# The down product of the first half of the tokens, turned round and in three float32r products

## The chip, the core and the metric

The kernel runs on one core of one Trainium2 chip. The metric is the device time of one execution in microseconds; three runs of the kernel before gave a median of 156.71 us (156.7 to 156.9). PE is TensorE, DVE is VectorE, ACT is ScalarE, POOL is GpSimd, SP is the queue engine that issues the DMAs.

## The reference

1024 tokens (4 batches of 256, 128 features) go through a cross attention over 1601 keys and then through a routed feed-forward part with 8 experts, 2 of them per token:

```
x = x + xattn(layernorm(x), ctx_1024, Wq, bq, Wk, bk, Wv, bv)
x = x + ffn(layernorm(x))

flat = hidden.reshape(B * S, H)
scores = softmax(flat @ router_weight.T + router_bias)
topk_w, topk_idx = top_k(scores, 2)
gu = einsum('th,ehn->ten', flat, gate_up_proj) + gate_up_bias
gate = minimum(gu[..., :I], 7.0);  up = clip(gu[..., I:], -7.0, 7.0)
act = (up + 1.0) * gate * sigmoid(gate * 1.702)
down = einsum('tei,eih->teh', act, down_proj) + down_bias
out = (take(down, topk_idx) * topk_w).sum(axis=1)
```

H is 128 and I is 256. All is float32.

## The kernel before

The tokens are eight tiles of 128, in two halves of four tiles (512 tokens). The attention goes tile by tile; its last tile overlaps the start of the feed-forward part. That part computes every expert for every token, and gives the experts that a token did not choose the weight 0. It is cut into 16 steps: four pairs of experts, and in each pair four steps (`PAIR_STEPS`), both experts for the first half of the tokens (k = 0, 1) and then both for the second (k = 2, 3). The first pair and the last are written out, the two in the middle are a hardware loop on every engine (`Fori`).

One step is:
- `gate_up` on PE: four groups (gate and up, each for two halves `ih` of the hidden features) of three float32r matmuls with 512 tokens streaming (`three`: high by high, high by low, low by high), into four PSUM banks S. The weights' high and low parts (`w_hi`, `w_lo`) are made by DVE one pair ahead, in the steps k = 2, 3.
- `silus` and `ups` on ACT: S with its bias into `gate` (it lies in `keysT_sb`) and `up` in SBUF, per `ih`.
- `clip_ups` and `product` on DVE: the clip of up, and gate by up into `act_t` (it lies in `xT` for even steps and in `act_odd` for odd ones).
- `down` on PE: for each token tile two float32 matmuls with the tile of `act_t` as the loaded weights and 128 columns of the down weights streaming; the tokens come out on the partitions. A float32 matmul is two passes in the trace. The result lies in the PSUM bank T0 or T1.
- `scale_y` on ACT: T by the routing weight of each token (per partition, `w_scaled`) into `y_sb` (it lies in `xn2`); `add_expert` on POOL: into `x1`.

The order on each engine is written out by hand. PE does the down product of step s, then gate_up of step s + 2. ACT and DVE go in step order. The routing of the second half (softmax, comparison of experts, weights) is on DVE between the products of steps 2 and 3, with a power operation on POOL for the exponentials. The biases of the down product are added as one product of the routing weights (turned by `transpose_weights`, copied by `copy_wT`) with `db_sb`, in `routed_bias`, into the banks O and M.

## Time and profile before

| | |
|---|---|
| runs, median | 156.71 us |
| profiled execution | 156.96 us |
| its span, first to last instruction | 155.2 us |
| PE busy | 149.2 us (96%) |
| PEld (weight loads) | 136.0 us |
| DVE busy | 103.2 us |
| ACT busy | 100.8 us |
| POOL busy | 49.8 us |
| granted TensorE clock | 1.000 |

The span is shorter than the profiled execution's time, since the time also holds what lies before the first and behind the last instruction. Busy times are of one engine each and overlap. An operation's recorded duration is a little longer than the distance at which the next one of its engine can follow.

### The profile page before, as it was taken

To read this page: it belongs to the slowest core of one execution; us is meant where nothing else is said; L and a number is where in the kernel's file an instruction comes from. 1 tells how busy PE (TensorE), PEld (TensorE's weight loads), DVE (VectorE), ACT (ScalarE), POOL (GpSimd) and SP (SyncE) were. 2 spreads that over 40 slices of the span, in tenths; PEclk is the share of its full clock that TensorE was granted. 3 is DMA by queue.
4 is the path that set the end of the run, shared out by engine and by line. 5 is a ranking of instruction groups with operands and counts; after the bars stand their busy time and mean duration, and the time that the engine had idled before them with its cause. 6 is when DMAs were issued, how large, how long until landed. Compare 5 with 4: busy or idle time off the path is not lost.

```text
span 155.2 us, 3023 instructions
## 1 busy us (share of the span) xinstructions
PE 149.2 (96%) x1004; PEld 136.0 (88%) x1004; DVE 103.2 (66%) x288; ACT 100.8 (65%) x205; POOL 49.8 (32%) x49
## 2 busy tenths in 40 slices
PE   7998799999999999999999999999999999999993
PEld 7988699999999999989988888788888888887892
DVE  0668958386859595963683899957654377552773
ACT  3183878657484736468866656957788677779450
POOL 1356529243505300210067643312333321233020
PEclk9999999999999999999999999999999999999999
DMA  4979999700000000000000000000000000000022
GB/s 116 371 292 404 388 401 384 225 1 4 0 2 0 4 0 0 4 0 2 0 0 4 0 0 0 0 4 0 2 0 0 0 0 0 0 4 0 4 68 68
DMA packets 5909, 10.69 MB, mean 69 GB/s; under 512 B 380, under 2 KB 3080, under 8 KB 5896
## 3 DMA queue, kind: packets, MB, share of 16 engines
q1 hardware_dynamic: 4968, 10.00, 17.9%
q10 hardware_dynamic: 928, 0.53, 1.2%
q8 instruction: 7, 0.11, 0.3%
q14 instruction: 6, 0.05, 0.1%
HBM read 10.00 MB, written 0.52 MB: 68 GB/s over the span
## 4 chain that ended last, share of the span: by engine, by line
PE 78%; DVE 10%; POOL 4%; ACT 3%; issue 3%; DVEq 0%
PE T L1147 14%; PE O L1041 13%; PE S L944 11%; PE S L946 10%; PE S L945 10%; PE T L1025 6%; PE S L951 3%; POOL ex L309 2%; DVE xT L847 2%; DVE up L838 1%; PE S L1147 1%; DVE w_lo L779 1%; DVE sc L631 1%; ACT pr L419 1%; POOL rstd L287 1%
## 5 line engine op out<-in xcount | busy, mean ns | idle before, releaser
L838 DVE TENSOR_SCALAR up<-up 128x512 f32<-128x512 f32 x32 | 13.9, 434 | 24.7 <-ACT up L504 24.7
L350 POOL TENSOR_TENSOR x<-x,xn 128x512 f32<-128x512 f32 x13 | 17.3, 1331 | 38.6 <-ACT xn L524 38.6
L427 ACT ACTIVATE pT<-T 128x512 f32<-128x512 f32 (+1 forms) x32 | 15.4, 513 | 18.4 <-PE T L1025 18.4
L524 ACT ACTIVATE xn<-T,w_scaled 128x128 f32<-128x128 f32 x56 | 16.1, 374 | 17.2 <-PE T L1147 14.1
L944 PE MATMUL S<-x_hi,w_hi 128*128 128x512 f32 x64 | 26.8, 419 | 0.2 <-DVE w_lo L779 0.2
L1041 PE MATMUL O<-pT,ctx_sb 128*128 128x128 f32 (+1 forms) x208 | 25.9, 275 | 0.2 <-ACT pT L427 0.2
L945 PE MATMUL S<-x_lo,w_hi 128*128 128x512 f32 x64 | 25.3, 395 | 0.0
L946 PE MATMUL S<-x_hi,w_lo 128*128 128x512 f32 x64 | 25.3, 395 | 0.0
L1041 PEld LDWEIGHTS O<-pT,ctx_sb 128*128 128x128 f32 (+1 forms) x208 | 24.6, 192 | 0.6 <-ACT pT L427 0.5
L631 DVE TENSOR_SCALAR_CACHE_REDUCE sc<-S,clip_hi 128x400 f32<-128x400 f32 (+1 forms) x32 | 18.9, 630 | 8.7 <-PE S L946 8.5
L498 ACT ACTIVATE keysT_sb<-S,gate_bias 128x512 f32<-128x512 f32 x32 | 22.7, 708 | 1.7 <-PE S L946 1.6
L504 ACT ACTIVATE up<-S,up_bias 128x512 f32<-128x512 f32 x32 | 22.5, 704 | 0.0
L287 POOL TENSOR_TENSOR rstd<-ve,minus_half 128x2 f32<-128x2 f32 (+1 forms) x7 | 7.5, 1076 | 36.7 <-DVE ve L674 27.6
L317 POOL TENSOR_TENSOR ct_lo<-keysT_sb,ct_hi 128x400 fp32r<-128x400 f32 (+1 forms) x12 | 12.5, 1060 | 14.0 <-ACT ct_hi L410 14.0
L1147 PEld LDWEIGHTS T<-dn_sb,xT 128*128 128x128 f32 x128 | 15.4, 192 | 0.9 <-issue 0.4
L1147 PE MATMUL T<-dn_sb,xT 128*128 128x128 f32 (+1 forms) x128 | 15.8, 276 | 0.2 <-DVE xT L847 0.2
L1025 PE MATMUL T<-ident,pr 128*128 128x128 f32 (+1 forms) x104 | 15.1, 274 | 0.6 <-ACT pr L419 0.6
L946 PEld LDWEIGHTS S<-x_hi,w_lo 128*128 128x128 f32 x64 | 12.0, 188 | 3.0
L1147 PEld LDWEIGHTS T<-dn_sb,act_odd 128*128 128x128 f32 x112 | 13.6, 191 | 1.0 <-DVE act_odd L847 0.4
L944 PEld LDWEIGHTS S<-x_hi,w_hi 128*128 128x128 f32 x64 | 12.1, 189 | 2.5 <-DVE w_lo L779 0.4
L1147 PE MATMUL T<-dn_sb,act_odd 128*128 (+1 forms) x112 | 14.0, 277 | 0.2 <-DVE act_odd L847 0.2
L945 PEld LDWEIGHTS S<-x_lo,w_hi 128*128 128x128 f32 x64 | 12.1, 189 | 2.1
(127 smaller groups left out, 248.4 us busy)
## 6 DMA issues: line engine op xcount, KB each, us to landing
keysT_sb<-in_ctxT SPq DMA_DIRECT2D x3, 801.0 KB, 9.9
...
```

What stands on the lines that cost most here:

```text
L350: nc.gpsimd.tensor_tensor(acc, acc, y_sb[:, k % 2, :], ALU.add).then_inc(y_added, 1)
L498: nc.scalar.activation(gate[:, k % 2, ih, :], S[2 * ih][:], ACT.Silu, bias=gate_bias[:, bass.ds(col + ih, 1)], scale=ALPHA).then_inc(silu_ ...
L504: nc.scalar.activation(up[:, k % 2, ih, :], S[2 * ih + 1][:], ACT.Relu, bias=up_bias[:, bass.ds(col + 2 + ih, 1)]).then_inc(up_ready, 1)
L524: ins = nc.scalar.activation(y_sb[:, k % 2, t * DIM:(t + 1) * DIM], T[k % 2][:, t * DIM:(t + 1) * DIM], ACT.Copy, scale=w_scaled[:, bass.d ...
L631: nc.vector.tensor_scalar(sc[:, n % 2, c0:c0 + w], S[c][:, 0:w], clip_hi[:, n:n + 1], None, ALU.min, ALU.max, accum_out=row_max[:, n, c:c ...
L838: nc.vector.tensor_scalar(up[:, k % 2, ih, :], up[:, k % 2, ih, :], 2.0 * LIMIT, 1.0 - LIMIT, ALU.min, ALU.add).then_inc(up_clipped, 1)
L944: nc.tensor.matmul(dst, a_hi, b_hi, start=True, stop=False)
L945: nc.tensor.matmul(dst, a_hi, b_lo, start=False, stop=False)
L946: return nc.tensor.matmul(dst, a_lo, b_hi, start=False, stop=True)
L1025: ins = nc.tensor.transpose(T[bank][0:rows, (t - t0) * P:(t - t0 + 1) * P], pr[:, n % 2, t * P:t * P + rows], ident[:])
L1041: ins = nc.tensor.matmul(O[:, q * P:(q + 1) * P], ctx_sb[b][0:rows, t, :], pT[0:rows, t, :], start=(t == 0), stop=(t == KT - 1))
L1147: ins = nc.tensor.matmul(dst, act_t[k % 2][:, ih, t * P:(t + 1) * P], dn_sb[:, bass.ds((e * 2 + ih) * DIM, DIM)], start=(ih == 0), stop=(i ...
```

## The change

For the first half of the tokens (steps k = 0, 1) the down product is turned: the down weights are the loaded ones, and all 512 tokens stream. It is done in float32r from high and low parts: low weights by high act, high by high (each for both `ih`), then high weights by low act, six matmuls of 128x512 (`down_turned`). For this ACT makes the high parts of act (`act_high`, into `ct_hi`) and of the down weights (`down_high`, into `g_hi`); POOL makes the low part of act for `ih` = 0 and of the down weights, DVE the low part of act for `ih` = 1 (`act_low`, both engines have one, into `ct_lo`; `down_low`, into `g_lo`). The result has the tokens along the free axis. DVE weights it there (`weight_yT`) by rows of routing weights that lie on all partitions: they are written to DRAM from `wT` and read back by two broadcasting DMAs (`w_first` for the first two experts, `w_rest`). POOL adds these results in `yT`. At the end PE turns `yT` back with the identity and adds the bias of that half in the same PSUM bank (`turn_back`), ACT copies it and POOL adds it to `x1`. The second half of the tokens goes as before.

```diff
+        act_hi, act_lo = ct_hi, ct_lo
+        dn_hi, dn_lo = g_hi[:, 0:4 * DIM], g_lo[:, 0:4 * DIM]
+        w_first = ctx_sb[0][:].rearrange("p t d -> p (t d)")[:, 0:2 * HTOK]
+        w_rest = sc[:].rearrange("p b k -> p (b k)")[:, 0:(EXPERTS - 2) * HTOK]
+        yT = ctx_sb[1][:].rearrange("p t d -> p (t d)")[:, 0:HTOK]
...
+            sp.wait_ge(wT_copied, 1)
+            sp.dma_start(w_rows, wT[:, 0:HTOK]).then_inc(w_rows_out, 16)
...
+            sp.wait_ge(w_rows_out, 16)
+            sp.dma_start(w_first, w_rows[0:2].rearrange("e t -> (e t)").partition_broadcast(P)).then_inc(w_first_in, 16)
+            sp.dma_start(w_rest, w_rows[2:EXPERTS].rearrange("e t -> (e t)").partition_broadcast(P)).then_inc(w_rest_in, 16)
...
+            def act_low(i, k):
+                j = i * 2 + k
+                pool.wait_ge(act_hi_ready, j * 2 + 1)
+                nc.gpsimd.tensor_tensor(act_lo[k][:, 0:HTOK], act_t[k][:, 0, :], act_hi[k][:, 0:HTOK].bitcast(F32),
+                                        ALU.subtract).then_inc(act_lo0_ready, 1)
+            def down_low(i):
+                nc.gpsimd.tensor_tensor(dn_lo, dn_sb[:, bass.ds(i * (4 * DIM), 4 * DIM)], dn_hi.bitcast(F32),
+                                        ALU.subtract).then_inc(dn_lo_ready, 1)
...
+                if h == 0:
+                    pool.wait_ge(yT_weighted, i * 2 + k + 1)
+                    acc = yT
+                else:
+                    pool.wait_ge(y_scaled, i * 2 + k - 1)
...
+                nc.gpsimd.tensor_tensor(acc, acc, y_sb[:, k % 2, :], ALU.add).then_inc(y_added, 1)
...
+            pool.wait_ge(o_done, 2)
+            nc.gpsimd.memset(yT, 0.0).then_inc(yT_blank, 1)
+            pool.wait_ge(dn_hi_ready, 1)
...
+            router_exponentials(2)
+            act_low(0, 1)
+            router_exponentials(3)
+            add_expert(0, 0)
...
+            down_low(1)
             with pool.Fori(1, PAIRS - 1) as i:
-                for k in range(4):
-                    add_expert(i * 4 + k, k)
...
+                act_low(i, 0)
+                add_expert(i - 1, 3)
+                act_low(i, 1)
+                add_expert(i, 0)
+                add_expert(i, 1)
+                add_expert(i, 2)
+                down_low(i + 1)
...
+            def act_high(i, k, ih):
+                act.wait_ge(act_ready, (i * 4 + k) * 2 + ih + 1)
+                nc.scalar.activation(act_hi[k][:, ih * HTOK:(ih + 1) * HTOK], act_t[k][:, ih, :],
+                                     ACT.Copy).then_inc(act_hi_ready, 1)
+            def down_high(i):
+                nc.scalar.activation(dn_hi, dn_sb[:, bass.ds(i * (4 * DIM), 4 * DIM)], ACT.Copy).then_inc(dn_hi_ready, 1)
...
-            with act.Fori(1, PAIRS - 1) as i:
-                for k in range(4):
-                    scale_y(i * 4 + k, k, i * 2 + PAIR_STEPS[k][0])
-                    s = k + 2
-                    e, h = PAIR_STEPS[s % 4]
...
+            with act.Fori(0, PAIRS - 1) as i:
+                expert(i * 4 + 2, 2, i * 8 + 0)
+                expert(i * 4 + 3, 3, i * 8 + 4)
+                act.wait_ge(route_ready, 2)
+                scale_y(i, 2, lambda: down_high(i + 1))
+                expert(i * 4 + 4, 0, i * 8 + 8)
+                act_high(i + 1, 0, 0)
+                act_high(i + 1, 0, 1)
+                scale_y(i, 3)
+                expert(i * 4 + 5, 1, i * 8 + 12)
+                act_high(i + 1, 1, 0)
+                act_high(i + 1, 1, 1)
+            copy_wT(1)
...
+            def act_low(i, k):
+                dve.wait_ge(act_hi_ready, (i * 2 + k) * 2 + 2)
+                nc.vector.tensor_tensor(act_lo[k][:, HTOK:2 * HTOK], act_t[k][:, 1, :],
+                                        act_hi[k][:, HTOK:2 * HTOK].bitcast(F32), ALU.subtract).then_inc(act_lo1_ready, 1)
+            def weight_yT(i, k):
+                step = i * 4 + k
+                dve.wait_ge(y_done, step + 1)
+                if isinstance(i, int) and i == 0:
+                    dve.wait_ge(w_first_in, 16)
+                    weights = w_first[:, k * HTOK:(k + 1) * HTOK]
+                else:
+                    dve.wait_ge(w_rest_in, 16)
+                    dve.wait_ge(y_added, step - 1)
+                    weights = w_rest[:, bass.ds(i * (2 * HTOK) + (k - 2) * HTOK, HTOK)]
...
                 clip_ups(step, k, 0)
                 product(step, k, 0)
                 clip_ups(step, k, 1)
-                if split is not None:
-                    split_w_hi(split, k % 2, step + 1)
+                if split:
+                    split_w_hi(i * 2 + k, k % 2, step + 1)
                 product(step, k, 1)
-                if split is not None:
-                    split_w_lo(split, k % 2)
+                if k == 1 or k == 2:
+                    weight_yT(i, k - 1)
+                if k < 2:
+                    act_low(i, k)
+                if split:
+                    split_w_lo(i * 2 + k, k % 2)
...
             product(1, 1, 1)
+            act_low(0, 1)
...
             split_w_lo(2, 0)
+            weight_yT(0, 0)
...
             product(3, 3, 1)
+            weight_yT(0, 1)
...
+            def down_turned(i, k):
+                step = i * 4 + k
+                if isinstance(i, int) and i == 0:
+                    pe.wait_ge(t_free[k], T_TOTAL[k])
                 else:
-                    pe.wait_ge(y_scaled, step - 1)
+                    pe.wait_ge(y_scaled, i * 2 + k - 1)
+                pe.wait_ge(dn_lo_ready, i + 1)
+                hi = [dn_hi[:, (k * 2 + ih) * DIM:(k * 2 + ih + 1) * DIM] for ih in range(2)]
+                lo = [dn_lo[:, (k * 2 + ih) * DIM:(k * 2 + ih + 1) * DIM] for ih in range(2)]
+                a_hi = [act_hi[k][:, ih * HTOK:(ih + 1) * HTOK] for ih in range(2)]
+                a_lo = [act_lo[k][:, ih * HTOK:(ih + 1) * HTOK] for ih in range(2)]
+                for ih in range(2):
+                    pe.wait_ge(act_hi_ready, (i * 2 + k) * 2 + ih + 1)
+                    nc.tensor.matmul(T[k][:], lo[ih], a_hi[ih], start=(ih == 0), stop=False)
+                    nc.tensor.matmul(T[k][:], hi[ih], a_hi[ih], start=False, stop=False)
+                pe.wait_ge(act_lo0_ready, i * 2 + k + 1)
+                nc.tensor.matmul(T[k][:], hi[0], a_lo[0], start=False, stop=False)
+                pe.wait_ge(act_lo1_ready, i * 2 + k + 1)
+                nc.tensor.matmul(T[k][:], hi[1], a_lo[1], start=False, stop=True).then_inc(y_done, 1)
...
+            def turn_back():
+                pe.wait_ge(y_added, STEPS - 2)
+                for t in range(HALF):
+                    bias_matmul(0, t, False)
+                    ins = nc.tensor.matmul(BIAS[0][:, t * DIM:(t + 1) * DIM], yT[:, t * P:(t + 1) * P], ident[:],
+                                           start=False, stop=True)
+                ins.then_inc(half0_done, 1)
...
                 for k in range(4):
-                    down(i * 4 + k, k, i * 2 + PAIR_STEPS[k][0])
+                    down_step(i, k)
...
+            down_turned(i, 0)
+            for ih in range(2):
+                gate_up(i * 4 + 2, 2, ih, i * 2 + 1)
+            routed_bias()
+            down_turned(i, 1)
+            for ih in range(2):
+                gate_up(i * 4 + 3, 3, ih, i * 2 + 2)
+            turn_back()
+            down(i, 2)
+            down(i, 3, tiles_apart=True)
```

POOL, one turn of its loop over pairs. Before, the four adds, each behind the scaling of its step (x is `x1`, xn is `y_sb`):

```order
L350 TENSOR_TENSOR x<-x,xn 128x512 [waits y_added,y_scaled]
L346 REGISTER_ALU
L350 TENSOR_TENSOR x<-x,xn 128x512 [waits y_added,y_scaled]
L346 REGISTER_ALU
L350 TENSOR_TENSOR x<-x,xn 128x512 [waits y_added,y_scaled]
L346 REGISTER_ALU
L350 TENSOR_TENSOR x<-x,xn 128x512 [waits y_added,y_scaled]
```

And now, where ct_lo is the low part of act, g_lo that of the down weights, and ctx_sb is `yT`:

```order
L363 TENSOR_TENSOR ct_lo<-xT,ct_hi 128x512 [waits act_hi_ready]
L377 ISA
L380 ISA [waits y_scaled]
L383 TENSOR_TENSOR x<-x,xn 128x512 [waits y_added]
L362 ISA
L363 TENSOR_TENSOR ct_lo<-act_odd,ct_hi 128x512 [waits act_hi_ready]
L380 REGISTER_ALU [waits yT_weighted]
L383 TENSOR_TENSOR ctx_sb<-ctx_sb,xn 128x512 [waits y_added]
L374 REGISTER_ALU
L380 REGISTER_ALU [waits yT_weighted]
L383 TENSOR_TENSOR ctx_sb<-ctx_sb,xn 128x512 [waits y_added]
L380 REGISTER_ALU [waits y_scaled]
```

Behind these stand a last add into x1 and the low part of the next pair's down weights: seven operations of 128x512 instead of four, and the add of the pair before's last step now comes between the two low parts.

DVE, the first two steps of a pair in its loop. Before:

```order
L838 TENSOR_SCALAR up<-up 128x512 [waits up_ready]
L847 SCALAR_TENSOR_TENSOR xT<-keysT_sb,up 128x512 [waits y_done,silu_ready,up_clipped]
L837 ISA
L838 TENSOR_SCALAR up<-up 128x512 [waits up_ready]
L847 SCALAR_TENSOR_TENSOR act_odd<-keysT_sb,up 128x512 [waits y_done,silu_ready,up_clipped]
L837 REGISTER_ALU
L838 TENSOR_SCALAR up<-up 128x512 [waits up_ready]
L847 SCALAR_TENSOR_TENSOR act_odd<-keysT_sb,up 128x512 [waits y_done,silu_ready,up_clipped]
```

And now, from the second half of the first step on (xn<-T,sc is the weighting of the step before):

```order
L905 TENSOR_SCALAR up<-up 128x512 [waits up_ready]
L914 SCALAR_TENSOR_TENSOR xT<-keysT_sb,up 128x512 [waits y_done,silu_ready,up_clipped]
L919 ISA
L920 TENSOR_TENSOR ct_lo<-xT,ct_hi 128x512 [waits act_hi_ready]
L904 ISA
L905 TENSOR_SCALAR up<-up 128x512 [waits up_ready]
L914 SCALAR_TENSOR_TENSOR act_odd<-keysT_sb,up 128x512 [waits y_done,silu_ready,up_clipped]
L904 REGISTER_ALU
L905 TENSOR_SCALAR up<-up 128x512 [waits up_ready]
L914 SCALAR_TENSOR_TENSOR act_odd<-keysT_sb,up 128x512 [waits y_done,silu_ready,up_clipped]
L934 ISA [waits y_added,w_rest_in,y_done]
L934 SCALAR_TENSOR_TENSOR xn<-T,sc 128x512
```

Each low part waits for ACT's second split of its step and stands ahead of the next step's clips; the weighting of step 0 stands behind the products of step 1, that of step 1 behind those of step 2 and ahead of `w_lo`.

## Rows read from the trace of the kernel before

**Rows 1.** The page, part 4: the chain that ended last, by engine.

```profile
PE 78%; DVE 10%; POOL 4%; ACT 3%; issue 3%; DVEq 0%
```

**Rows 2.** Busy time by stretch: pair 1, pair 2, last pair to the end.

```profile
core 0: us, PE busy (x) PEld busy (x) DVE busy (x) ACT busy (x) POOL busy (x), PEclk, DMA share, GB/s
...
97.50:114.57 17.07, 16.76 (x96) 14.44 (x97) 11.51 (x21) 13.17 (x32) 4.99 (x4) 1.00 0.00 1
114.57:132.92 18.35, 18.35 (x114) 16.18 (x113) 10.62 (x20) 13.88 (x33) 5.16 (x5) 1.00 0.00 0
132.92:155.20 22.28, 19.59 (x130) 17.01 (x128) 12.46 (x26) 11.99 (x27) 4.07 (x4) 1.00 0.08 25
```

**Rows 3.** Order of time, PE, one step (start us, us, engine, line, operation).

```profile
107.27 0.48 PE L944 MATMUL S<-x_hi,w_hi 128*128 128x512 f32 x1
...
110.15 1.95 PE L1147 MATMUL T<-dn_sb,xT 128*128 x16
...
111.85 0.47 PE L944 MATMUL S<-x_hi,w_hi 128*128 128x512 f32 x1
```

**Rows 4.** Order of time, ACT, POOL and DVE, the same step.

```profile
108.69 0.71 ACT L498 ACTIVATE keysT_sb<-S,gate_bias 128x512 f32<-128x512 f32 x1
108.89 1.29 POOL L350 TENSOR_TENSOR x<-x,xn 128x512 f32<-128x512 f32 x1 [3.22 <-ACT xn L524]
...
109.26 0.72 ACT L504 ACTIVATE up<-S,up_bias 128x512 f32<-128x512 f32 x1
...
110.01 0.46 DVE L838 TENSOR_SCALAR up<-up 128x512 f32<-128x512 f32 x1 [1.39 <-ACT up L504]
...
110.50 0.69 DVE L847 SCALAR_TENSOR_TENSOR act_odd<-keysT_sb,up 128x512 f32<-128x512 f32 x1
111.17 0.43 DVE L838 TENSOR_SCALAR up<-up 128x512 f32<-128x512 f32 x1
111.51 0.42 DVE L774 CAST w_hi<-gu_sb 128x512 fp32r x1
```

**Rows 5.** Order of time, POOL and DVE, where both read SBUF.

```profile
26.57 1.65 POOL L317 TENSOR_TENSOR ct_lo<-keysT_sb,ct_hi 128x400 fp32r<-128x400 f32 x1
...
27.39 0.87 DVE L806 TENSOR_SCALAR gate_bias<-more_sb 128x32 f32<-128x32 f32 x1
...
89.12 0.69 DVE L847 SCALAR_TENSOR_TENSOR xT<-keysT_sb,up 128x512 f32<-128x512 f32 x1
89.12 1.83 POOL L350 TENSOR_TENSOR x<-x,xn 128x512 f32<-128x512 f32 x1 [1.17 <-ACT xn L524]
...
89.72 1.78 DVE L779 TENSOR_TENSOR w_lo<-gu_sb,w_hi 128x512 fp32r<-128x512 f32 x1
...
99.10 1.30 POOL L350 TENSOR_TENSOR x<-x,xn 128x512 f32<-128x512 f32 x1 [2.08 <-ACT xn L524]
99.11 1.83 DVE L847 SCALAR_TENSOR_TENSOR xT<-keysT_sb,up 128x512 f32<-128x512 f32 x1
```

**Rows 6.** The same view, where a DVE operation wasn't lengthened.

```profile
40.01 2.04 POOL L317 TENSOR_TENSOR ct_lo<-keysT_sb,ct_hi 128x400 fp32r<-128x400 f32 x2 [2.39 <-ACT ct_hi L410]
...
40.02 0.42 DVE L684 TENSOR_TENSOR x_lo<-M,x_hi 128x256 fp32r<-128x256 f32 x1
...
83.82 2.90 POOL L309 TENSOR_TENSOR ex<-e_base,logit 128x16 f32<-128x16 f32 x1 [0.91 <-DVE logit L703]
...
85.84 0.69 DVE L847 SCALAR_TENSOR_TENSOR xT<-keysT_sb,up 128x512 f32<-128x512 f32 x1
```

**Rows 7.** Groups by line: ACT's copy from SBUF nearest in size.

```profile
L448 ACT ACTIVATE ct_hi<-keysT_sb 128x578 fp32r<-128x578 f32 x1 | 0.7, 677 | 0.0
```

**Rows 8.** Order of time, PE, gate_up of step 5.

```profile
97.62 0.50 PE L944 MATMUL S<-x_hi,w_hi 128*128 128x512 f32 x1 [0.21 <-DVE w_lo L779]
```

**Rows 9.** The same view, last pair: down product of step 12, bias product.

```profile
138.10 1.95 PE L1147 MATMUL T<-dn_sb,xT 128*128 128x128 f32 x16
...
142.78 1.15 PE L1166 MATMUL M<-db_sb,wT 8*128 8x128 f32 x8
```

168 lines of the change are left out of this document (88 added, 80 removed).

## The prediction

> **What bounds the kernel now.** I read the chain of waits first, then the stretches by engine, then the order of time in one pair of experts. The chain that ended last is 78% TensorE [rows 1]. In the feed-forward part one pair of experts (four steps: both experts for the first token half, then both for the second) takes 18.35 us, and TensorE is busy for all of it, VectorE for 10.62 us, ScalarE for 13.88, GpSimd for 5.16; the granted clock is 1.00, the higher level [rows 2]. So after its first pair this stage is bound by TensorE. One step there is 4.58 us (107.27 to 111.85): the twelve float32r matmuls of gate and up take 2.88 us, 0.24 each, and the sixteen passes of the float32 down product 1.70 us [rows 3]. What hides behind it: ScalarE's activations start 0.57 us apart (108.69, 109.26), VectorE's clips and products follow, GpSimd adds for 1.29 us and stands still otherwise [rows 4]. In the first pair the routing of the second half lies between VectorE's products, and TensorE waits for the w_lo behind them until 97.62 [rows 8].
>
> **What the change saves.** A turned down product is six matmuls of 128x512 in float32r: 6 x 0.24 = 1.44 instead of 1.70, 0.26 saved. The 0.24 includes a slow first matmul behind float32 work (recorded with 0.48), so 0.26 is the lower end; without it I take up to 0.35. Eight such steps: 2.1 to 2.8 us, if nothing else is late.
>
> **What it adds, per pair.** ScalarE: four splits of act and one of the down weights. A 128x578 copy from SBUF takes 0.68 us [rows 7]; for 512 columns I take 0.6 of duration and 0.5 of pace, so 2.5 us; two scale_y (1.0 us each in pace) go. ScalarE's 13.88 us stay well below 18, so I cost this at nothing as load. It costs as latency: ScalarE works in order and now waits for VectorE's product before it can split it, and the next step's silus stand behind that. VectorE: two act_low and two weightings, each like the product, 0.69 recorded, 0.60 in pace: 2.4 us. GpSimd: seven operations of 1.29 instead of four: 9.0 us for 5.2.
>
> **What they share.** This is the term that decides. Where GpSimd and VectorE both read SBUF, one waits for the other. The add of 99.10 to 100.40 held a product issued at 99.11 until it had taken 1.83 us instead of 0.69, and it ended 0.54 behind the add's end. At 89.12 the product came first: the add took 1.83 instead of 1.29, and the w_lo behind it 1.78. It isn't only for two inputs: a tensor_scalar of only 128x32, issued at 27.39, took 0.87 us and ended just behind GpSimd's subtraction (26.57 to 28.22) [rows 5], where a clip with sixteen times the elements takes 0.43 [rows 4]. It isn't so for VectorE operations that read PSUM: x_lo took 0.42 us at 40.02, inside two subtractions on GpSimd [rows 6]. So clips, casts, products, w_lo and act_low are held; the two weightings, which read T, are not. The held time of an add, from the row at 99.11: it frees about 0.15 us before its recorded end, so 1.14.
> Sum for one pair: GpSimd 7 x 1.14 = 8.0; VectorE 12 operations with two inputs (8 products, 2 w_lo, 2 act_low) x 0.54 = 6.5; 10 with one (8 clips, 2 casts) x 0.3 = 3.0. Together 17.5 us. TensorE's own work of a pair falls to 18.35 - 2 x 0.26 to 0.35 = 17.7. Before, the same sum was 4.6 + 5.4 + 3.0 = 13.0, and GpSimd's adds fell into the 1.39 us before 110.01 in which VectorE waited for up: the add of 108.89 met no more than the first clip (0.46 for 0.43) [rows 4]. Now the operations are let go by events in the midst of VectorE's runs: act_low on GpSimd by the first split, while VectorE does the second clip and product; the add of expert 0 by VectorE's weighting, before its act_low; the add of expert 1 by the second weighting, before w_lo; the add behind scale_y and then down_low meet the products of step 3 and the first clip of the next pair. Such a sum cannot be packed without gaps.
> A rule of the Trainium skill bears on it. The page "SBUF — State Buffer", section "SBUF: two separate sides", has a port pair that VectorE and GpSimd take in turns, held for the full instruction. The trace agrees in kind, but not in length: the add frees early by 0.15 us, and the power operation of 2.90 us at 83.82 didn't hold the product at 85.84 (0.69) at all [rows 6]. By the full length the pair's sum would be 1 us more and the forecast some 3 us later; the measured rows decide, and I keep 1.14.
>
> **One pair.** I set VectorE's loop in order with these durations, let whichever operation is issued first go first, and put time 0 at the first clip of the pair. VectorE: step 0 ends at 1.9; act_low waits for ScalarE's split and GpSimd's act_low, 3.6. ScalarE has meanwhile begun scale_y and the silus of step 1 late, so the first clip of step 1 is at 4.9, its product at 6.9, weighting 7.5, act_low (behind GpSimd's) 8.6. Step 2 begins behind the add, 9.7, and ends with w_lo at 13.1; step 3 behind the next add, 14.2; its second product behind the third, and w_lo behind down_low, about 19. TensorE gets the last w_lo only then. VectorE's own 11.8 us (8 x 0.34, 8 x 0.60, 2 x 0.34, 6 x 0.60) plus 7.2 us held or waiting: about 19.0 us a pair, and TensorE idle for over 1 us of them. The ends of this unknown: 17.7 (all hidden) and 11.8 + 7 x 1.14 + 0.8 = 20.6 (all seven held).
>
> **The sum**, against the profiled execution's own 156.96 us (span 155.2):
> - Until the first turned product: the bias product leaves (1.1 us by its like at 142.78) [rows 9], but the two lows and the later variance of the last batch push what follows by about as much. 0.
> - First pair, to the first clip of the second at 97.5: VectorE's chain with the routing sets it. Step 1's act_low waits for the last split, and the differences that GpSimd's power operation (2.90 us) needs stand behind it, 1 to 2 us later; two weightings add 1.2 us; holds by GpSimd move but stay about as many. So w_lo of expert 3 and gate_up at 97.62 [rows 8] come 0 to 2.6 us later, and the clip is held by the add of step 2 and down_low besides, up to 1.8. Ends 0 and +4.4; I take +2.6, past the middle, since all these instructions stand in VectorE's own order.
> - Two pairs from that clip to the first clip of the last pair: 17.07 + 18.35 = 35.4 before [rows 2], 2 x 19.0 = 38.0 after: +2.6. Ends 0 (2 x 17.7) and +5.8.
> - Last pair: 22.28 us from its first clip to the end [rows 2]. That clip is now nearer to its down product: by my order 3.0 us, where it was 5.2 (132.92 to 138.10) [rows 9], so -2.2. Two turned products save 0.6. turn_back adds a bias product (1.1) and four float32 turns (8 passes x 0.106 = 0.85), and step 13's act_low and ScalarE's copy of wT ahead of step 14 hold TensorE for about 1.0. The first half's output goes by ScalarE, GpSimd and the DMA while TensorE does 3.5 us of down products, and is hidden. Together 0.2; with ends -0.6 and +1.3 I take +0.4.
> Together +5.6: 162.6, and since the median of the runs (156.71) is 0.25 below the profiled one, 162.3. The order by hand taken word for word gives +7.0.
> The weights' way through DRAM is not in the sum: By my order wT is copied at about 81.5 and VectorE first wants the weights at about 92, and the rest of them (1.5 MB) a pair later; the DMA engines have nothing else to do there (share 0.00) [rows 2]. So 10 us hide the write and the first broadcast of 0.5 MB, and if these took longer the first weighting would wait by so much.
>
> **Rivals.**
> 1. The shared access is hidden, TensorE goes on bounding. For it: every GpSimd operation has slack of its own, and in the steady pairs of before the adds cost VectorE almost nothing. Against: 17.5 of 17.7 us. Eight products save 2.1 to 2.8, the turns cost 0.85 more than they save elsewhere: 154.8 to 155.5, I say 155.1.
> 2. The first pair and the tail lose, the loops break even because a hold falls into waits for ScalarE more often than in my order: 156.7 + 2.6 + 0.4 = 159.7, or down to 157.5 if the first pair loses little.
> 3. Slower by another cause: ScalarE. Its splits stand in line before silu; should each wait for a product 1.1 us behind the ups, twice per turned step, it has 13.9 + 2.5 - 2.3 + 4 = 18.1 us a pair, the old length. It decides from holds of 1 us on, which is my forecast's mechanism again; alone it gives 156.7 + 1.4 for the tail = 158.1.
> 4. It doesn't shorten the product: if the loads of 128x128 weights were not hidden behind 512 columns. Each of the twelve matmuls of gate and up has such a load and goes at 0.24, so hardly.
>
> **How the numbers follow.** Forecast 0.55, its own range 160 to 164.5. Rival 2 with 3: 0.20, 157 to 160. Rival 1: 0.20, 154.5 to 156. About no change: 0.05, where the losses of the first pair meet the gains. A measurement of this kernel can tell 0.2% from no change. Faster 0.21, same 0.05, slower 0.74. The range leaves out half of rival 1 at most and the end above 164.5.
>
> **What would show it.** In the pair by pair stretches: TensorE's busy time below the length, with waits for VectorE (act_lo, w_lo, act) that were not there; products and w_lo near 1.8 us beside GpSimd operations; a pair of about 19 us. Wrong: pairs of 17.6 us and TensorE busy throughout, or VectorE operations at 0.69 inside GpSimd's (then nothing is shared), or a pair lengthened while VectorE idles (then it is ScalarE's order).

## The result, and the profile after

The changed kernel takes 167.99 us (median of 4 runs, 167.33 to 168.81) where the kernel before takes 156.75 in the same comparison: ratio 1.0718, 95% interval 1.067 to 1.0766. It is 11.2 us slower. The forecast had the sign and the mechanism, but 162.3 us, and the measured time lies 3.5 us above the end of its range (164.5).

The profiled execution took 167.33 us, with a span of 165.6. The page's first part (busy time and share of the span) and its chain of waits by engine:

```profile
PE 152.9 (92%) x932; PEld 131.3 (79%) x932; DVE 123.4 (74%) x303; ACT 104.9 (63%) x194; POOL 71.3 (43%) x63
...
PE 38%; DVE 28%; issue 14%; ACT 8%; POOL 6%; DMA 2%; ACTq 1%; DVEq 1%; POOLq 0%
```

TensorE's share of the chain fell from 78% [rows 1] to 38%, VectorE's rose from 10% to 28%. To see where the time went, I cut both spans at the first clip of steps 4, 8 and 12. The busy time by stretch (length, then PE, PEld, DVE, ACT, POOL, clock, DMA) of the changed kernel, against [rows 2]:

```profile
79.00:99.60 20.60, 17.06 (x84) 14.41 (x85) 17.03 (x37) 11.61 (x23) 10.34 (x6) 0.92 0.29 103
99.60:120.43 20.83, 19.76 (x97) 14.84 (x96) 18.25 (x25) 15.50 (x31) 11.91 (x9) 1.00 0.01 2
120.43:140.41 19.98, 19.37 (x95) 14.66 (x94) 17.44 (x26) 14.89 (x30) 10.77 (x8) 1.00 0.00 0
140.41:165.60 25.19, 21.01 (x112) 16.04 (x110) 16.65 (x30) 11.99 (x23) 9.74 (x7) 1.00 0.08 22
```

| stretch | before | after | measured | predicted |
|---|---|---|---|---|
| up to the first clip of step 4 | 97.5 | 99.6 | +2.1 | +2.6 |
| two pairs, steps 4 to 11 | 17.1 + 18.3 | 20.8 + 20.0 | +5.4 | +2.6 |
| last pair to the end | 22.3 | 25.2 | +2.9 | +0.4 |
| span | 155.2 | 165.6 | +10.4 | +5.6 |

In the second pair (120.43 to 140.41) VectorE is now busy for 17.44 of 19.98 us, where it was busy for 10.62 of 18.35 [rows 2]. Its own work grew by only 2.4 us (to 12.98 us with GpSimd's work cut, in the first experiment); the rest is instructions that last longer. TensorE's 19.37 us are not all work: a matmul is recorded with 0.40 us where the next one can start 0.23 us later, so short waits between matmuls count as busy. In order of time, VectorE and GpSimd in that pair (start, duration, engine, line, operation, wait before it):

```profile
118.75 1.76 DVE L846 TENSOR_TENSOR w_lo<-gu_sb,w_hi 128x512 fp32r<-128x512 f32 x1
120.43 1.51 DVE L905 TENSOR_SCALAR up<-up 128x512 f32<-128x512 f32 x1
...
124.52 0.99 DVE L920 TENSOR_TENSOR ct_lo<-xT,ct_hi 128x512 fp32r<-128x512 f32 x1 [0.70 <-ACT ct_hi L584]
126.71 0.55 DVE L905 TENSOR_SCALAR up<-up 128x512 f32<-128x512 f32 x1 [1.20 <-ACT up L557]
...
128.96 0.68 DVE L934 SCALAR_TENSOR_TENSOR xn<-T,sc 128x512 f32<-128x512 f32 x1
...
130.99 1.19 DVE L905 TENSOR_SCALAR up<-up 128x512 f32<-128x512 f32 x1 [0.25 <-ACT up L557]
...
135.29 1.51 DVE L905 TENSOR_SCALAR up<-up 128x512 f32<-128x512 f32 x1
...
138.72 1.76 DVE L846 TENSOR_TENSOR w_lo<-gu_sb,w_hi 128x512 fp32r<-128x512 f32 x1
```

```profile
119.92 1.73 POOL L368 TENSOR_TENSOR g_lo<-dn_sb,g_hi 128x512 fp32r<-128x512 f32 x1
123.50 1.46 POOL L363 TENSOR_TENSOR ct_lo<-xT,ct_hi 128x512 fp32r<-128x512 f32 x1 [1.84 <-ACT ct_hi L584]
125.69 1.28 POOL L383 TENSOR_TENSOR x<-x,xn 128x512 f32<-128x512 f32 x1 [0.72 <-ACT xn L575]
128.72 1.46 POOL L363 TENSOR_TENSOR ct_lo<-act_odd,ct_hi 128x512 fp32r<-128x512 f32 x1 [1.76 <-ACT ct_hi L584]
130.14 1.76 POOL L383 TENSOR_TENSOR ctx_sb<-ctx_sb,xn 128x512 f32<-128x512 f32 x1
134.94 1.58 POOL L383 TENSOR_TENSOR ctx_sb<-ctx_sb,xn 128x512 f32<-128x512 f32 x1 [3.04 <-DVE xn L934]
138.36 1.58 POOL L383 TENSOR_TENSOR x<-x,xn 128x512 f32<-128x512 f32 x1 [1.84 <-ACT xn L575]
139.89 1.74 POOL L368 TENSOR_TENSOR g_lo<-dn_sb,g_hi 128x512 fp32r<-128x512 f32 x1
```

Read them side by side. Each long VectorE instruction is issued while a GpSimd one runs, and ends a little behind it: the clip of 135.29 (1.51 us for 0.42) is issued inside the add of 134.94 and ends at 136.80, 0.28 behind it. The w_lo of 138.72 is held by the add of 138.36, and as it lasts until 140.48, it is itself in the way of the down_low of 139.89, which then holds the next clip. So the holding works both ways, and one hold hands over to the next. How long a hold is follows from the rows: the held instruction needs its own time from about 0.15 us before GpSimd's recorded end. For the w_lo of 138.72 that gives 139.94 - 0.15 + 0.68 = 140.47, and it ended at 140.48; the act_low of 124.52, issued late in GpSimd's, was held for only 0.3 us. The weighting of 128.96, which reads T, is issued inside GpSimd's act_low of 128.72 and isn't held at all (0.68 us). The sum of the lengthening in this pair is 1.1 + 0.3 + 0.3 + 0.1 + 0.8 + 1.1 + 1.1 = 4.8 us (clip of 120.43, the two act_low, of which the second, 1.00 us at 129.74, isn't shown, clips 126.71, 130.99 and 135.29, w_lo of 138.72).

TensorE meets it in the turned product:

```profile
123.56 0.42 PE L1240 MATMUL T<-ct_hi,g_lo 128*128 128x512 f32 x1
...
124.54 0.50 PE L1240 MATMUL T<-ct_hi,g_lo 128*128 128x512 f32 x1 [0.32 <-ACT ct_hi L584]
124.88 0.40 PE L1241 MATMUL T<-ct_hi,g_hi 128*128 128x512 f32 x1
125.11 0.40 PE L1243 MATMUL T<-ct_lo,g_hi 128*128 128x512 f32 x1
125.56 0.49 PE L1245 MATMUL T<-ct_lo,g_hi 128*128 128x512 f32 x1
```

Without waits the next matmul starts 0.23 us after one (124.88 to 125.11), so from the first start to the last it should be 1.15 us. It was 2.0 (123.56 to 125.56): with the last matmul's own 0.23 they took 2.2 us, more than the 1.70 us of the product that they replace [rows 3]. 0.5 us of it is the wait for ScalarE's second split and 0.2 us the one for VectorE's held act_low. The next gate_up starts another 0.4 us later, at 126.15. With GpSimd's work cut (the first experiment) the same six go without a gap, 1.39 us from the first to the next gate_up where it is 2.59 here:

```profile
118.45 0.40 PE L1240 MATMUL T<-ct_hi,g_lo 128*128 128x512 f32 x1
...
119.84 0.40 PE L1035 MATMUL S<-x_hi,w_hi 128*128 128x512 f32 x1
```

The first pair holds a thing that I had not seen:

```profile
85.27 3.01 POOL L327 TENSOR_TENSOR ex<-e_base,logit 128x16 f32<-128x16 f32 x1 [1.12 <-DVE logit L770]
...
88.32 0.18 DVE L781 TENSOR_REDUCE esum<-ex 128x4 f32<-128x32 f32 x1 [2.06 <-POOL ex L327]
...
91.27 0.68 DVE L934 SCALAR_TENSOR_TENSOR xn<-T,ctx_sb 128x512 f32<-128x512 f32 x1
...
92.00 2.94 PE L1256 MATMUL T<-dn_sb,xT 128*128 128x128 f32 x16 [2.98 <-DVE xn L934]
```

TensorE stood still for 2.98 us ahead of step 2's down product, and then its granted clock was lower: 0.65 and 0.51 on average in the two stretches below. By single microseconds it was 0.98 from 92 to 93 and 0.50, the lower of its two levels, from there to about 96.4. The sixteen passes took 2.94 us for 1.95.

```profile
92.00:95.20 3.20, 3.20 (x18) 3.10 (x19) 3.13 (x6) 0.00 (x0) 1.38 (x1) 0.65 0.00 0
95.20:96.40 1.20, 1.20 (x4) 0.96 (x3) 1.10 (x6) 0.16 (x1) 0.00 (x0) 0.51 0.00 0
```

### The profile page after: what moved, and what is told of

It reads as the page before. It is cut to its first block, busy times and chain, and to the rows that moved or that the text cites. A ratio compares the mean times of both kernels' runs of the same rounds, so it can differ in the third digit from the quotient of the medians.

```text
span 165.6 us, 2957 instructions
## 1 busy us (share of the span) xinstructions
PE 152.9 (92%) x932; PEld 131.3 (79%) x932; DVE 123.4 (74%) x303; ACT 104.9 (63%) x194; POOL 71.3 (43%) x63
## 4 chain that ended last, share of the span: by engine, by line
PE 38%; DVE 28%; issue 14%; ACT 8%; POOL 6%; DMA 2%; ACTq 1%; DVEq 1%; POOLq 0%
PE O L1132 12%; DVE up L905 11%; PE T L1116 6%; PE S L1035 4%; PE S L1037 4%; PE S L1036 4%; DVE act_odd L914 3%; ACT up L557 2%; DVE xT L914 2%; DVE xn L934 2%; DVE w_lo L846 2%; DMA x_sb<-in_x 2%; POOL ex L327 2%; POOL rstd L305 1%; PE T L1256 1%
## 5 line engine op out<-in xcount | busy, mean ns | idle before, releaser
L905 DVE TENSOR_SCALAR up<-up 128x512 f32<-128x512 f32 x32 | 21.6, 676 | 8.0 <-ACT up L557 8.0
L551 ACT ACTIVATE keysT_sb<-S,gate_bias 128x512 f32<-128x512 f32 x32 | 22.3, 696 | 2.9 <-PE S L1037 2.5
L383 POOL TENSOR_TENSOR ctx_sb<-ctx_sb,xn 128x512 f32<-128x512 f32 x8 | 12.5, 1558 | 16.9 <-DVE xn L934 16.9
L472 ACT ACTIVATE pr<-sc,neg_max 128x1601 f32<-128x1601 f32 x8 | 13.0, 1629 | 0.2 <-DVE sc L707 0.2
L575 ACT ACTIVATE xn<-T,w_scaled 128x128 f32<-128x128 f32 x24 | 7.1, 366 | 9.5 <-DVE w_scaled L834 6.4
L1116 PEld LDWEIGHTS T<-ident,pr 128*128 128x128 f32 (+1 forms) x104 | 12.2, 141 | 1.2 <-ACT pr L472 0.7
L1035 PE MATMUL S<-ct_hi,g_hi 128*128 128x400 f32 (+1 forms) x32 | 12.4, 388 | 0.4 <-POOL ct_lo L343 0.4
L914 DVE SCALAR_TENSOR_TENSOR xT<-keysT_sb,up 128x512 f32<-128x512 f32 x16 | 11.9, 745 | 0.6
```

The source lines that it names most:

```text
L472: nc.scalar.activation(pr[:, n % 2, 0:KEYS], sc[:, n % 2, 0:KEYS], ACT.Exp, bias=neg_max[:, n:n + 1], accum_out=row_sum[:, n:n + 1]).then_ ...
L551: nc.scalar.activation(gate[:, k % 2, ih, :], S[2 * ih][:], ACT.Silu, bias=gate_bias[:, bass.ds(col + ih, 1)], scale=ALPHA).then_inc(silu_ ...
L905: nc.vector.tensor_scalar(up[:, k % 2, ih, :], up[:, k % 2, ih, :], 2.0 * LIMIT, 1.0 - LIMIT, ALU.min, ALU.add).then_inc(up_clipped, 1)
L914: nc.vector.scalar_tensor_tensor(act_t[k % 2][:, ih, :], gate[:, k % 2, ih, :], SILU_LIMIT, up[:, k % 2, ih, :], ALU.min, ALU.mult).then_i ...
L1035: nc.tensor.matmul(dst, a_hi, b_hi, start=True, stop=False)
L1116: ins = nc.tensor.transpose(T[bank][0:rows, (t - t0) * P:(t - t0 + 1) * P], pr[:, n % 2, t * P:t * P + rows], ident[:])
```

## The experiments

In the "narrow" kernels below an engine's operations are cut to 8 of their 512 columns. They leave all waits and their order in place and take away only the time that the operations need; what they compute is left out but for these columns.

**Which engine's added work costs the time.** Three runs, one engine each. GpSimd: act_low, down_low and add_expert narrow.

```diff
-nc.gpsimd.tensor_tensor(acc, acc, y_sb[:, k % 2, :], ALU.add)
+nc.gpsimd.tensor_tensor(acc[:, 0:8], acc[:, 0:8], y_sb[:, k % 2, 0:8], ALU.add)
```
(and the same for the low parts)

> The changed kernel with all of GpSimd's operations of the feed-forward loop (two low parts of act, that of the down weights, four adds) cut to 8 of 512 columns; the rest of those columns is left out, every wait stays. If VectorE is late because GpSimd's reads hold it: a steady pair of experts (first clip of step 8 to that of step 12, 19.98 us in the changed kernel) falls to 17.6 to 18.0, TensorE's own work, and the whole to 160 to 162 us. If VectorE's own added work or ScalarE's order is what counts: the pair stays at 19.3 or more, the whole at 166 or more.

Measured: 157.91 us, ratio to before 1.0078 (1.0057 to 1.0099), which is 2.1 us below my range for it. Of the 11.2 us 10.1 are gone, and they go from every stretch: 2.4 us from the first pair (its end is at 97.18, where it was at 99.59), 3.7 and 2.4 from the two in the loop, 1.2 from the last. Busy time of its second pair, and its group of clips (line, form, count, then busy time, mean ns of one, idle time before):

```profile
114.36:131.91 17.55, 17.55 (x95) 14.86 (x94) 12.98 (x25) 14.87 (x30) 2.60 (x7) 1.00 0.00 0
```
```profile
L905 DVE TENSOR_SCALAR up<-up 128x512 f32<-128x512 f32 x32 | 13.6, 425 | 13.2 <-ACT up L557 13.2
```

VectorE does the same 32 clips at the same widths, and their mean is 425 ns; in the changed kernel it is 676:

```profile
L905 DVE TENSOR_SCALAR up<-up 128x512 f32<-128x512 f32 x32 | 21.6, 676 | 8.0 <-ACT up L557 8.0
```

TensorE is busy for the whole pair again, which is 17.55 us long: 0.8 shorter than before, so the turned product does save its 0.4 us when nobody is late. VectorE's and ScalarE's added operations, which are whole here, cost the pair nothing.

VectorE: its act_low and weight_yT narrow.

```diff
-nc.vector.scalar_tensor_tensor(y_sb[:, k % 2, :], T[k % 2][:], 1.0 / ALPHA, weights,
+nc.vector.scalar_tensor_tensor(y_sb[:, k % 2, 0:8], T[k % 2][:, 0:8], 1.0 / ALPHA, weights[:, 0:8],
```

> The changed kernel with VectorE's low part of act and its weighting cut to 8 of 512 columns (left out: the other columns). These are 2.4 us a pair of VectorE's own. If VectorE's work and what holds it make the pair: 19.98 falls by about 2 us to 17.8 to 18.3. If ScalarE's order (split behind product, silus behind split) makes it, these two stand beside the path and the pair loses less than 0.8.

Measured: 164.33 us, ratio 1.0488 (1.0427 to 1.0549). The second pair is 18.77 us, 1.2 shorter than after, although VectorE's busy time fell by 3.2 (17.44 to 14.26). That lies between my two expectations and fits neither. VectorE is still held: a product issued at 118.71, inside down_low, took 1.57 us for 0.69. The half of it that came back shows how much VectorE's own added work matters as long as GpSimd's is there. In this run the clock was 0.93 in the last stretch, so the whole time understates it; the pair at clock 1.00 is the number to use.

```profile
117.59:136.36 18.77, 18.31 (x94) 14.54 (x94) 14.26 (x25) 14.71 (x30) 10.12 (x8) 1.00 0.00 0
136.36:163.30 26.94, 23.05 (x121) 18.25 (x120) 14.23 (x29) 13.10 (x24) 10.19 (x8) 0.93 0.07 20
```

ScalarE: act_high and down_high narrow.

```diff
-nc.scalar.activation(act_hi[k][:, ih * HTOK:(ih + 1) * HTOK], act_t[k][:, ih, :],
+nc.scalar.activation(act_hi[k][:, ih * HTOK:ih * HTOK + 8], act_t[k][:, ih, 0:8],
```

> The changed kernel with ScalarE's splits of act and of the down weights cut to 8 columns (left out: the rest), waits kept. ScalarE's order: if the splits' own time on it counts (five of 0.5 us a pair), the pair loses 2 us or more. If the held access does: each split is waited for by VectorE only at its low part (0.70 us idle twice a pair) and by the next ups, so the pair loses 0.5 to 1.2.

Measured: 172.92 us, ratio 1.1036 (1.1014 to 1.1058). Less work on ScalarE made the kernel 4.9 us slower than the changed one; neither expectation had that sign. Part of the 4.9 us goes with a lower clock (0.92 in the first of the two loop pairs, 0.94 in the last stretch). The waits and their order are the same, so the reason must lie in when things happen. Its second pair, at clock 1.00, is 22.41 us long, 2.4 more than after:

```profile
122.07:144.48 22.41, 19.26 (x95) 14.77 (x94) 19.50 (x25) 12.58 (x29) 11.33 (x8) 1.00 0.00 0
```
```profile
124.43 0.21 ACT L584 ACTIVATE ct_hi<-xT 128x8 fp32r<-128x8 f32 x1 [2.77 <-DVE xT L914]
...
124.72 1.29 POOL L363 TENSOR_TENSOR ct_lo<-xT,ct_hi 128x512 fp32r<-128x512 f32 x1 [1.42 <-ACT ct_hi L584]
...
124.77 1.78 DVE L914 SCALAR_TENSOR_TENSOR xT<-keysT_sb,up 128x512 f32<-128x512 f32 x1
...
129.11 0.54 DVE L905 TENSOR_SCALAR up<-up 128x512 f32<-128x512 f32 x1 [1.59 <-ACT up L557]
```

The split is ready 0.4 us earlier, so GpSimd's act_low starts at 124.72, 0.05 us ahead of VectorE's second product, and holds it for 1.1 us. In the changed kernel the product was issued at 123.13, 0.4 us ahead of GpSimd's act_low (123.50), and took 0.69, and only the less urgent act_low of 124.52 was held by 0.3. ScalarE's second split (126.59) waits for the held product, and with it, in order, the silus of the next step, so that its first clip comes 7.0 us behind the one of step 8 instead of 6.3. The same happens in step 9 (a product of 1.78 us at 130.75). This is direct evidence that it is the overlap that costs, and not the amount of work.

**Additions or low parts.** GpSimd's narrow run again, half of it at a time: first only the three subtractions of a pair, then only the four additions.

```diff
-nc.gpsimd.tensor_tensor(dn_lo, dn_sb[:, bass.ds(i * (4 * DIM), 4 * DIM)], dn_hi.bitcast(F32),
+nc.gpsimd.tensor_tensor(dn_lo[:, 0:8], dn_sb[:, bass.ds(i * (4 * DIM), 8)], dn_hi[:, 0:8].bitcast(F32),
```

> Of GpSimd's three kinds of work in a pair only the subtractions (two act_low, one down_low) are cut to 8 columns, so act_lo of the first row half and dn_lo are left out but for 8 columns; the four additions stay whole. Theory (VectorE is held whatever the GpSimd operation is, and a hold is paid where VectorE is the one waited for): in the steady pair of the changed kernel the three subtractions lengthen VectorE's instructions by 0.3 + 0.3 + 1.1 = 1.7 us, the additions by 0.75 + 1.1 + 1.1 + 0.1 = 3.0 us. Without the subtractions the pair goes from 20.0 to 18.6 to 19.4 us, and the run to 162.5 to 165 us. Rival (not the hold, but the lateness of the low parts, for which the turned product waits): all of what the narrow GpSimd gave comes back here, pair 17.5 to 17.9 us and the run 157.5 to 159 us.

Measured: 162.81 us, ratio 1.0376 (1.0352 to 1.04), second pair 18.58 us.

> The mirror of the run before: the four additions of a pair are cut to 8 columns (the sums are left out but for these), the three subtractions stay whole. Theory of the hold: the additions' 3.0 us of held time is the larger part, pair 18.2 to 18.9 us, run 161 to 164 us. Rival of the late low parts: nothing comes back, pair 19.6 to 20.0 us and the run 167 to 168 us. If the two halves don't add up to the 2.4 us a pair that both together gave, it is because one held instruction moves where the next falls.

Measured: 160.72 us, ratio 1.0243 (1.0223 to 1.0264), second pair 18.11 us.

The pair gained 1.4 us by the first and 1.9 by the second, together 3.3 where both at once gave 2.4. The rival "the low parts are late for TensorE" would have put all of it on the subtractions and nothing on the additions; it falls, since the larger part is the additions, which no engine waits for in the changed kernel's loop (the waits of 99.6 to 140.4 list none for an addition, and 0.7 us in all for GpSimd's low parts). That the two gains overlap has two reasons that these runs don't part: where one kind is taken away the other has fewer holds to hand over, and no pair can be shorter than TensorE's own 17.55 us. With narrow additions the pair came out 0.1 and the whole 0.3 us below what I expected.

**Holds where nobody is waiting.** The kernel before, with three whole subtractions a pair added on GpSimd (their result isn't used, nothing else is changed):

```diff
+                    if k == 0 or k == 3:
+                        extra_low(i * 4 + k + 1, k, i * 3 - 2 + (k > 0) * 2)
                     add_expert(i * 4 + k, k)
+                    if k == 2:
+                        extra_low(i * 4 + k + 1, k, i * 3 - 1)
```

> The kernel before with three more subtractions of 128x512 a pair on GpSimd in its loop, from the down weights into an unused buffer, each let go in the midst of VectorE's clips and products, as the low parts are now. They add nothing to the result. If a hold always lengthens the kernel: 3 x 1.1 us a pair, 6 to 7 us in all. If holds count only where VectorE has no slack (here it idles 1.4 to 2.3 us a step): within 1 us of the kernel before, with products or w_lo near 1.8 us in the trace.

Measured: 156.88 us, ratio 0.9999 (0.9987 to 1.0012).

```profile
114.54:132.89 18.35, 18.35 (x114) 16.17 (x113) 13.68 (x21) 13.88 (x33) 9.47 (x8) 1.00 0.00 0
```

```profile
117.06 1.67 DVE L862 SCALAR_TENSOR_TENSOR xT<-keysT_sb,up 128x512 f32<-128x512 f32 x1
```

VectorE's busy time in this pair went from 10.62 us [rows 2] to 13.68: it was held for 3.1 us (three products of 1.41 to 1.67 us and a clip of 1.03), and the pair stayed at 18.35. So a hold costs nothing by itself. It costs where VectorE has no slack, and the change took that away: its busy time without holds rose from 10.6 to 13.0 us (the pair with GpSimd narrow), while the waits for ScalarE's splits were put into its chain.

**The low parts on VectorE alone.** act_low of both halves is one VectorE operation of 128x1024, none on GpSimd; the arithmetic is whole.

```diff
-                nc.vector.tensor_tensor(act_lo[k][:, HTOK:2 * HTOK], act_t[k][:, 1, :],
-                                        act_hi[k][:, HTOK:2 * HTOK].bitcast(F32), ALU.subtract)
+                nc.vector.tensor_tensor(act_lo[k][:, 0:2 * HTOK], act_t[k].rearrange("p c t -> p (c t)"),
+                                        act_hi[k][:, 0:2 * HTOK].bitcast(F32), ALU.subtract)
```

> The changed kernel with the low parts of act made by VectorE alone, one operation of 1024 columns a step (about 1.15 us for 0.69), and GpSimd's two a pair gone; nothing is left out. VectorE gets 1.1 us more of its own a pair and loses two holds. Held access: a hold costs 0.6 to 1.1, so the pair stays equal or falls, 19.0 to 20.0. Own load: the pair grows to 20.7 to 21.1.

Measured: 169.56 us, ratio 1.0809 (1.0744 to 1.0874), second pair 20.21 us. No gain, between the two expectations. The wide operation takes 1.23 us where the held narrow one took 0.99, and the add then meets the first clip of step 10 (1.42 us for 1.19). This doesn't tell the theories apart; it shows that one exchange only moves the hold. Of the 2.2 us between the two profiled spans 1.3 lie in its last stretch (26.50 us for 25.19), where the clock was 0.94.

**The first pair.** weight_yT(0, 0) right behind step 2's first product instead of behind w_lo, ahead of the wait for the routing's sum.

```diff
             product(2, 2, 0)
+            weight_yT(0, 0)
             sum_exponentials(1)
...
             split_w_lo(2, 0)
-            weight_yT(0, 0)
```

> The changed kernel with one instruction moved: VectorE's weighting of step 0 stands before the sum of the second half's exponentials, where VectorE idles for 2.06 us, and no longer behind w_lo. If the bank T0 that this weighting frees is what TensorE waits for (2.98 us before the down product of step 2, then 3 to 4 us at the lower clock): the down product starts at 90.9 (its act is there) and not 92.0, the clock's fall is shorter or gone, the first clip of step 4 comes 1 to 3 us earlier, and the whole is 1 to 2.5 us shorter. If the routing chain on VectorE alone sets the first pair, the stall goes but the clip of step 4 stays within 0.7 us.

Measured: 166.79 us, ratio 1.0653 (1.0612 to 1.0694), so 1.2 us less than the changed kernel.

```profile
87.12 0.69 DVE L934 SCALAR_TENSOR_TENSOR xn<-T,ctx_sb 128x512 f32<-128x512 f32 x1 [0.55 <-DMA ctx_sb<-w_rows]
...
89.17 0.38 PE L1256 MATMUL T<-dn_sb,xT 128*128 128x128 f32 x2
91.75 1.49 PE L1256 MATMUL T<-dn_sb,xT 128*128 128x128 f32 x11 [2.20 <-DVE xT L914]
```

TensorE can start two passes at 89.17, but then waits for VectorE's second product, which stands behind the same sum, so the rest begins hardly sooner (91.75 for 92.00). The first clip of step 4 is 0.7 us earlier (98.85), and the clock stayed at 1.00 here. I can't part the two: the clock also stayed at 1.00 in the profile of the next kernel, behind a standstill of 2.99 us, and the first clip of step 4 was at 99.83 there, no earlier than after (99.59). So the lower clock in the changed kernel's first pair cost its loop little, since VectorE sets that clip, and the gain comes rather from the order of VectorE's instructions. It hangs on GpSimd as well: with GpSimd's work cut, the clip of step 4 stands at 97.18 with the early weighting and without it. One thing that the move changes is which instruction GpSimd's add of step 0 holds: in the changed kernel a `ties` of the routing (1.49 us for 0.42), here the shorter `prob` (0.83 for 0.19). The weights' way through DRAM, free in the changed kernel, costs 0.55 us here.

**The end.** Bias products and turns of turn_back in two groups (in banks BIAS[0] and BIAS[1], the bias added to x1 apart), instead of one by one:

```diff
                 for t in range(HALF):
-                    bias_matmul(0, t, False)
-                    ins = nc.tensor.matmul(BIAS[0][:, t * DIM:(t + 1) * DIM], yT[:, t * P:(t + 1) * P], ident[:],
-                                           start=False, stop=True)
+                    ins = bias_matmul(0, t, True)
+                ins.then_inc(db_done, 1)
...
+                for t in range(HALF):
+                    ins = nc.tensor.matmul(BIAS[1][:, t * DIM:(t + 1) * DIM], yT[:, t * P:(t + 1) * P], ident[:],
+                                           start=True, stop=True)
```

> The changed kernel with another end: the four bias products of the first half stand together behind the last gate_up and VectorE adds them into x1 (0.7 us), and the four turns stand together behind the wait for yT, into the other bank. Same arithmetic. If the alternation of 8-row and 128-row matmuls cost the time (3.23 us for 16 passes, where 1.08 + 0.85 was expected) and the wait for yT is now filled: 1.5 to 1.9 us less. If the passes cost 0.2 us because of what they read: below 0.5 us less.

Measured: 167.93 us, ratio 1.0706: nothing. turn_back by itself became shorter. In the changed kernel it ran from 155.84 to 159.07, 3.23 us, two passes at a time:

```profile
155.84 0.48 PE L1272 MATMUL O<-db_sb,wT 8*128 8x128 f32 x2
...
156.25 0.49 PE L1288 MATMUL O<-ident,ctx_sb 128*128 128x128 f32 x2
```

Grouped it took 2.07 us (157.44 to 159.51). But the profile of this run has the clock at 0.50 from 152.5 to 155.6, behind a wait of 1.01 us for the copy of the transposed weights:

```profile
150.42 1.12 PE L1276 MATMUL M<-db_sb,wT 8*128 8x128 f32 x8 [1.01 <-ACT wT L568]
...
157.44 1.15 PE L1276 MATMUL O<-db_sb,wT 8*128 8x128 f32 x8
158.52 1.16 PE L1295 MATMUL M<-ident,ctx_sb 128*128 128x128 f32 x8
```
```profile
152.50:155.60 3.10, 3.10 (x9) 2.35 (x8) 2.69 (x5) 0.72 (x2) 0.89 (x1) 0.50 0.00 0
```

Matmuls of 128x512 follow one another at 0.43 us in that stretch (153.41 to 153.84) and not at 0.23. Over eight of them that is about 1.5 us, more than the 1.2 that the grouping gained.

The grouping changed two things at once. Before it every turn also added onto the bias that the product just ahead of it had written in the same bank; grouped, the turns go alone into another bank. So the 1.2 us are those of both together, and the alternation by itself is not shown to be the cause.

The three edits with whole arithmetic together (weighting early, turn in groups, low parts on VectorE):

> The changed kernel with the three mends together: weighting of step 0 early, the end regrouped, the low parts of act on VectorE alone. Nothing is left out. If the three act in different places, the gains add up: 2.5 to 5 us below the changed kernel, 163 to 165.5, still above the kernel before, since the pair stays near 19.5.

Measured: 165.79 us, ratio 1.0592 (1.0546 to 1.0639); last stretch 23.9 us at clock 1.00. That is 0.3 us above my range, since the pairs stayed at 21.1 and 20.2 us and not near 19.5. To keep the low parts on GpSimd and take the wait away as well, routed_bias goes behind the second turned product of the last pair:

```diff
             for ih in range(2):
                 gate_up(i * 4 + 2, 2, ih, i * 2 + 1)
-            routed_bias()
             down_turned(i, 1)
+            routed_bias()
```

> The changed kernel with whole arithmetic and the same three mends: weight_yT(0, 0) right behind the second product, the turning back in two groups, routed_bias behind the second turned product of the last pair, so that TensorE does not wait 1.0 us for the copy of the transposed weights. Theory (the end lost what the grouping gave because the clock fell behind that wait): 1.2 + 1.0 + 1.0 us off 168.0, 164.5 to 165.8 us, with the clock at full in the last 30 us. Rival (the end is set by held VectorE instructions and not by TensorE): only the first mend counts, 166.5 to 167.3 us. In both cases slower than the kernel before.

Measured: 164.76 us, ratio 1.0506 (1.0484 to 1.0528), 3.2 us under the changed kernel. The last stretch is 23.31 us for 25.19, at clock 1.00 in both, and the pairs are as they were (20.86 and 19.98). So 1.9 us of the end lay in the order of TensorE's own instructions and not in the holds.

**What is left when nothing holds.** The same three edits with GpSimd's loop work narrow:

> All of GpSimd's loop work cut to 8 columns (sums and low parts left out but for these), and beside it the three mends that leave the arithmetic as it is: weight_yT(0, 0) right behind the second product, the turning back in two groups, and routed_bias behind the second turned product of the last pair. Theory (three causes, each with its own price: the held VectorE 6 to 7 us over the loop, the late weighting 0.7 to 1.2 us, the end 1 to 2 us): from the 157.9 us of the narrow GpSimd alone to 155.0 to 156.3 us, at or just under the kernel before. Rival (TensorE's own work bounds what is left, with 17.5 us a pair against 18.35 and a longer end, so the mends only move idle time): 157.2 to 157.9 us.

Measured: 156.46 us, ratio 0.998 (0.9963 to 0.9997). With GpSimd's work all but gone, the design just meets the kernel before. The second pair is 17.54 us, the last stretch 22.89, where before it was 22.28 [rows 2]. The result is 0.2 us above my range for it.

No version with whole arithmetic beats the kernel before; the best is 5% slower.

## Why the prediction was right and where it was wrong

**Right in kind.** "What they share" decided: the GpSimd narrow run takes 10.1 of the 11.2 us away, VectorE's operations on SBUF were the lengthened ones, and the weightings, which read T, were not held (0.68 us at 128.96, inside a GpSimd operation). TensorE's own pair was put at 17.7 us and is 17.55. Rival 1, all of it hidden, was put at 155.1 us; the design doesn't get there even with GpSimd's work taken away and its first pair and end mended (156.46). Rival 2, loops that break even, falls with pairs of 20.8 and 20.0 us. Rival 4 falls with the 0.23 us of a turned matmul. Rival 3, ScalarE as an own cause, has half a truth: its splits pass VectorE's lateness on to the next step's silus, but its load costs nothing where VectorE isn't held (17.55 us a pair with all splits whole).

**"Two pairs from that clip": +2.6 taken, +5.4 measured.** This step and the next, "Last pair", are where the sum failed. This one is the largest error, and a size, not the mechanism. I took 19.0 us from an order by hand, with 7.2 us held or waiting on top of VectorE's 11.8. Measured in the second pair are 19.98 us, of which VectorE lost 4.8 to holds and 2.2 to waits for ScalarE (0.70, 1.20 and 0.25), with some 1.2 of gaps that my pace figures left out. So the 7.2 was met there (7.0), and the missing 1 us is the gaps. The first of the two pairs had the same gaps and waits, but 5.6 us of holds, and so 20.83. Two of my details were off, and in the second pair their errors cancelled, which is luck. In the steady pair no product was held; clips, w_lo and act_low were, since GpSimd's operations are let go when a product is through. And I let an add hold VectorE for 1.14 us once; I hadn't allowed in this order that a held w_lo delays the next GpSimd operation in turn (1.73 us for down_low), which then holds the clip behind it. The first of the two pairs starts with three held instructions in a row:

```profile
98.01 1.66 DVE L846 TENSOR_TENSOR w_lo<-gu_sb,w_hi 128x512 fp32r<-128x512 f32 x1
99.59 1.50 DVE L905 TENSOR_SCALAR up<-up 128x512 f32<-128x512 f32 x1
101.23 1.56 DVE L914 SCALAR_TENSOR_TENSOR xT<-keysT_sb,up 128x512 f32<-128x512 f32 x1
```
I had set both pairs alike, though the one before had been 17.07 and not 18.35 [rows 2], so the pairs weren't alike to begin with. The upper bound (+5.8) did hold it; the value between the ends was too near the middle.

**"Last pair": +0.4 taken, +2.9 measured**, outside its own bounds (-0.6 to +1.3). Three terms of it failed, by about 2.6 us together. turn_back was priced as grouped passes, 1.1 + 0.85 us, but one by one it takes 3.23 (1.3 more); grouped it takes 2.07. The first of the two turned products, priced at 1.44, took 2.2 until the next gate_up (143.89 to 146.12), 0.8 more, with waits for VectorE's act_low and for ScalarE. And the way from the clip to it was 3.5 us (140.41 to 143.89) and not 3.0. I left out that this pair's VectorE work is held as in any other. "Hold TensorE for about 1.0", the wait for wT's copy, is there with 1.0. By the experiments, the narrow GpSimd alone takes 1.2 us off this stretch, the two edits to TensorE's order 1.9.

**"First pair": +2.6 taken, +2.1 measured**, near in size, for a partly wrong reason. I had counted the later routing and the two weightings as well as the holds; but with GpSimd's work cut, and both of these still there, the clip of step 4 is at 97.18 and the whole +2.1 is gone. The rows show where: a w_lo of 1.66 us (98.01), a `ties` of 1.49 and an act_low of 1.00 us (83.69) were lengthened by 1.0, 1.1 and 0.3. So GpSimd's holds made it, the terms for the order came to nothing, and the nearness of the sum is partly luck. I also hadn't seen that TensorE would wait 2.98 us for bank T behind the weighting and then go on at a lower clock. The early weighting gained 0.7 us here and 1.2 in the whole, while the clock by itself, at 1.00 in the kernel with the turn in groups, gained nothing (99.83 for 99.59); the wait that remains there (2.20 us) is for VectorE's product. The part until the first turned product, put at 0, came to +0.7 us (it starts at 79.77, where the down product before started at 79.10, behind a wait of 0.72 us for the last batch's layernorm) and is contained in the +2.1.

The range was too narrow because its upper end was the sum of the values taken (+5.6) plus 2.2, while the ends of the terms added up to +11.5. The measured +10.4 lies near that sum, though not because each term came out at its end: the first pair stayed under the value taken, the two pairs came near their end (+5.4 of +5.8) and the last pair went past its own. The terms did share a cause, since the cut of GpSimd's work shortens every stretch, so their misses could not be expected to cancel.

What stays open: how much of the 20.0 us a better order of GpSimd's seven operations could win back with whole arithmetic; no such order was tried. And what makes the clock fall behind one stretch of waits and not behind another: the changed kernel's profile shows 1.00 behind its 1.02 us wait for wT's copy, the grouped one's 0.50 behind the same.
